# Spreading a statistics stream over sixteen turns of an image instead of twelve

## The chip, the cores and the metric

The kernel runs on one core of a Trainium2 chip. The metric is the device time of one execution in microseconds (us). The kernel before takes 6187.13 us, the median of 3 runs (6186.45 to 6190.99).

## The reference

The input x has 8 images of 32 channels by 512 by 512 pixels, float32. Two layers follow one another, each of the form x + layer(group norm of x); a group is two channels.

```python
def _gn(v, G=16, eps=1e-5):
    g = v.reshape(B_, G, C_ // G, H_, W_)
    m = jnp.mean(g, axis=(2, 3, 4), keepdims=True)
    s = jnp.var(g, axis=(2, 3, 4), keepdims=True)
    return ((g - m) / jnp.sqrt(s + eps)).reshape(v.shape)

# layer 0: 3x3 convolution on values quantised to int8, result quantised again
x_q = _quantize(x, S_X)
w_q = _quantize(weight, S_W)
acc = conv(x_q, w_q, padding=1)
out_q = clip(round((acc * (S_X * S_W) + bias) / S_OUT))      # times S_OUT
x = x + layer0(_gn(x))

# layer 1: 1x1 convolution, 5x5 pooled bins of it are the filter of a 5x5 depthwise convolution
x = x + layer1(_gn(x))
```

The mean and variance of a whole image must be known before the first value of this image can be quantised. That is why the first layer reads most of x twice.

## The kernel before, in words

The first layer is `quantised_conv`. An image is cut into N = 16 chunks of 2.1 MB (128 partitions by 8 rows by 512 float32), and one pass of a loop over n is a turn. Images are worked one after the other (`Fori` over b, the last image written out behind the loop). In turn n:

- SyncE (SP) and ScalarE (ACT) each issue the loads of half a chunk (L326) into one of eight slots `b_x`; a load waits until the store of the chunk that had the slot is complete. SP's loads run five turns ahead, and from n = 11 on they are chunks 0 to 5 of the next image.
- ACT quantises a chunk (L386), widens it to bf16 (L393) and rounds four results of the convolution (L401) into `b_q`, which has room for one chunk.
- TensorE (PE) does the convolution (L443 to L456).
- VectorE (DVE) adds the rounded result to the chunk (L521, two instructions), takes statistics of the sum for the second layer (L532, L536), and GpSimd (POOL) stores the chunk (L577).
- For the group norm of the next image, DVE takes bn_stats of its chunks too (L480). Four of its chunks (`RESIDENT`) are in their slots by then and are read there in turns 11 to 14. The other twelve are loaded once for this alone, by SP (L366), into `b_stream`, two halves of half a chunk each. A half is loaded again when DVE has read it. `TAKEN` says that these twelve are read in turns 0 to 11, one each.

In turn 14 the statistics are complete: DVE aggregates them (L484), PE sums over the partitions of a group (L255) behind its last convolution of the image, DVE forms spread and variance (L234 to L241), ACT a square root (L259) behind its last rounding of the image, DVE the scale (L490) and the shift (L491). The first L386 of the next image waits for L491. Behind turn 15 stands DVE's tail of an image (L542 to L554) with 20 chained links, each an instruction that waits for the one before it.

The order of the work is that of the code: each engine does its instructions in the order in which its loop issues them, and waits in between on semaphores. SP is one such queue for both kinds of load. DVE's add in turn n waits for ACT's rounding, ACT's next rounding waits for DVE's add, PE waits for ACT. The second layer (`depthwise`) begins when the first is over; the change doesn't touch it.

Of the kernel before, what the change touches and what calls it, by code (L numbers as in the profile page):

```python
# [27 lines left out]
RESIDENT = 4  # L28
XQ_SLOTS = 4
# [232 lines left out]
def quantised_conv(nc, nb, k, x, x1, own, sums):  # L262
# [4 lines left out]
    with ExitStack() as ctx:  # L267
        def sb(name, shape, dt):
            return ctx.enter_context(nc.sbuf_tensor(name, shape, dt))
# [8 lines left out]
        st_x = sb("b_stats_x", [P, N * JB, 6], F32)  # L278
        st = sb("b_stats", [P, NTUP, 6], F32)
# [34 lines left out]
        next_x = x[1:nb, :, :, :].rearrange("b c (n j r) w -> b n r c j w", j=JB, r=4)  # L314
        x1v = x1.rearrange("b (n j r) c w -> b n (r c) j w", j=JB, r=4)
# [28 lines left out]

        TAKEN = [[RESIDENT + n] if n < STREAMED else [] for n in range(N)]
        for j in range(RESIDENT):
            TAKEN[N - X_SLOTS + 3 + j].append(j)

        block = ctx.enter_context(nc.Block())

        @block.sync
        def _(sp):
            sem.start(sp)
            sp.wait_ge(padded, 1 + START)

            load_first(sp, (0, 1))

            def body(b, more):
                for n in range(N + 1):
                    load_ahead(sp, b, n + X_SLOTS - 3, more, (0, 1))  # L360
                    if more and n < STREAMED:
                        for h in range(2):

                            sp.wait_ge(stream_read[h], b * STREAMED + n + START)
                            for r in range(Q):
                                sp.dma_start(xs[C * r:C * r + C, h, :, :],  # L366
                                             next_x[b, RESIDENT + n, r, :, JB // 2 * h:JB // 2 * (h + 1), :]).then_inc(stream_loaded[h], 16)


            sp.wait_ge(first_read, N - AHEAD + START)  # L370
            with sp.Fori(0, nb - 1) as b:
                body(b, True)
            body(nb - 1, False)
# [96 lines left out]
        def _(dve):  # L470
# [4 lines left out]
            TAIL = 2 + 2 * NSEG + 1  # L475

            def take(tile, n, j0, rows):

                for j in range(rows):
                    last = dve.bn_stats(st_x[:, n * JB + j0 + j, :], tile[:, j, :])  # L480
                return last

# [10 lines left out]
            def body(b, more):  # L493
                tail = [0]

                def link(ins):
                    tail[0] += 1
                    ins.then_inc(chain, 1)
                    dve.wait_ge(chain, b * TAIL + tail[0] + START)

                for n in range(N):
                    s = n % X_SLOTS
                    for m in TAKEN[n] if more else ():
                        if m < RESIDENT:
                            dve.wait_ge(x_loaded[m], loads_at(b + 1, m) + START)
                            last = take(xt[:, m, :, :], m, 0, JB)
                        else:
                            for h in range(2):
                                dve.wait_ge(stream_loaded[h], b * (STREAMED * LOAD) + (m - RESIDENT + 1) * LOAD + START)
                                take(xs[:, h, :, :], m, JB // 2 * h, JB // 2).then_inc(stream_read[h], 1)  # L510
# [28 lines left out]
                    if more and n == N - 2:  # L539
                        gs.vector_variance(dve, b + 1)  # L540
# [16 lines left out]
            for i, n in enumerate([*range(AHEAD, N), *range(AHEAD)]):  # L557
                dve.wait_ge(x_loaded[n % X_SLOTS], LOAD * (i // X_SLOTS + 1) + START)
                last = take(xt[:, n % X_SLOTS, :, :], n, 0, JB).then_inc(first_read, 1)
# [5 lines left out]
            with dve.Fori(0, nb - 1) as b:  # L565
                body(b, True)
            body(nb - 1, False)
# [595 lines left out]
```

## Time and profile before

| | |
|---|---|
| median of 3 runs | 6187.13 us |
| the profiled execution, its time | 6187.55 us |
| its span in the profile | 6185.9 us |
| busy: PE, DVE, ACT, POOL | 79%, 85%, 54%, 14% |
| first image: scale known (L491) | at 129.9 us |
| last image: scale known | at 2323.0 us |
| last L386 of the first layer | starts at 2492.3 us |
| DVE, waiting for `b_stream` (L480) | 381.0 us in 151 waits |
| POOL, waiting in front of its stores (L577) | 2310.3 us |

The profiled execution took 0.4 us more than the median. Its span leaves out 1.65 us before and behind. The first layer fills about the first 42% of the span; the whole-span shares mix it with the second layer. So the first layer is read by stretches of an image.

### The profile page before, as it was taken

How to read it: one execution, taken by the hardware profiler on the slowest of the kernel's cores; microseconds unless marked ns; L12 is line 12 of the kernel's file. 1: busy time of each engine (PE TensorE's matmuls, PEld its weight loads, DVE VectorE, ACT ScalarE, POOL GpSimd, SP SyncE). 2: the span in 40 equal slices, each digit the busy share in tenths (PEclk: the TensorE clock that was granted, in tenths of full speed). 3: DMA queues.
4: the chain of work that ended last, by engine and by line, in shares of the span. 5: the costliest groups of instructions: out<-in, count | busy, mean ns of one | idle time of the engine just before them, and what ended most of it. 6: DMA issues, size and time to landing. Idle time of an engine off the chain costs nothing.

```text
span 6185.9 us, 112158 instructions
## 1 busy us (share of the span) xinstructions
PE 4916.9 (79%) x43630; PEld 3222.5 (52%) x43798; DVE 5284.7 (85%) x5934; ACT 3360.9 (54%) x2005; POOL 889.3 (14%) x1444
## 2 busy tenths in 40 slices
PE   1767676767676779349989989989899899899899
PEld 0111111111111112138878878878788788788787
DVE  6787878787878787659989989989899899899898
ACT  1656565646564649235545545545455455455454
POOL 0000000000000001102212212112112121122122
PEclk9888788878888889679999999999999999999999
DMA  8999999999999999389999999999999999999998
GB/s 259 301 280 307 287 300 287 303 286 294 299 301 298 297 286 299 100 182 257 244 251 251 250 252 252 251 249 257 246 260 243 256 255 250 256 249 251 252 255 195
DMA packets 617611, 1615.46 MB, mean 261 GB/s; under 512 B 81338, under 2 KB 82618, under 8 KB 580282
## 3 DMA queue, kind: packets, MB, share of 16 engines
q1 hardware_dynamic: 239298, 640.73, 41.7%
q0 software_dynamic: 162240, 537.03, 27.1%
q10 hardware_dynamic: 215488, 429.94, 25.8%
q8 instruction: 363, 5.95, 0.4%
q14 instruction: 222, 1.82, 0.1%
HBM read 1068.55 MB, written 538.84 MB: 260 GB/s over the span
## 4 chain that ended last, share of the span: by engine, by line
DVE 43%; issue 7%; DMA 3%; PE 2%; ACTq 1%; POOL 0%; SPq 0%; ACT 0%; DVEq 0%; another core or an unknown queue 0%; POOLq 0%
DVE c_z L1003 16%; DVE c_xr L1039 16%; DVE c_feat L1029 12%; DMA c_xr<-x_scratch 3%; PE c_tps L1083 1%; ACTq L859 1%; PE c_cps L1063 0%; POOL c_feat L922 0%; SPq L887 0%; PE c_cps L1065 0%; PE c_cps L1064 0%; ACT c_z L969 0%; DVEq L1002 0%; SPq L872 0%
## 5 line engine op out<-in xcount | busy, mean ns | idle before, releaser
L1083 PE MATMUL c_tps<-c_feat,c_tt 123*128 123x256 f16 (+1 forms) x20736 | 2377.0, 273 | 13.8 <-DVE c_xr L1039 10.7
L1083 PEld LDWEIGHTS c_tps<-c_feat,c_tt 123*128 123x128 f16 (+1 forms) x20736 | 1992.1, 97 | 275.0 <-issue 15.6
L987 ACT ACTIVATE c_feat<-c_cps 122x1024 f16<-122x1024 f32 x576 | 822.5, 1428 | 1352.1 <-PE c_cps L1065 1352.1
L1039 DVE SCALAR_TENSOR_TENSOR c_xr<-c_tps,c_xr 57x1024 f32<-57x1024 f32 (+1 forms) x1152 | 1403.2, 1218 | 158.6 <-DMA c_xr<-x_scratch 125.7
L443 PE MATMUL b_ps<-b_xq,w0main 128*128 128x512 bf16 x2904 | 918.4, 419 | 656.9 <-ACT b_q L401 484.5
L969 ACT ACTIVATE c_z<-c_x,c_rs 128x976 f16<-128x976 f32 x576 | 1156.6, 2008 | 275.5 <-PE c_tps L1083 169.1
L1003 DVE SCALAR_TENSOR_TENSOR c_z<-c_x,c_rs,c_z 128x976 f16<-128x976 f32 x576 | 1087.1, 1887 | 105.3 <-ACT c_z L969 92.9
L1063 PE MATMUL c_cps<-w_high,c_z 128*128 128x128 f16 x4608 | 822.1, 222 | 421.5 <-DVE c_z L1003 385.6
L936 POOL DMA_DIRECT2D out_dram<-c_xr x1152 | 667.4, 580 | 2892.5 <-DVE c_xr L1039 2827.9
L401 ACT ACTIVATE b_q<-b_ps,q_bias 128x1024 int8<-128x1024 f32 x512 | 549.2, 1115 | 813.8 <-DVE b_x L521 745.5
L456 PE MATMUL b_ps<-b_xq,w0edge 64*32 64x512 bf16 x3048 | 931.3, 416 | 0.0
L453 PE MATMUL b_ps<-b_xq,w0edge 64*32 64x512 bf16 x3048 | 929.3, 416 | 0.0
L443 PEld LDWEIGHTS b_ps<-b_xq,w0main 128*128 128x128 bf16 x3072 | 227.1, 101 | 1307.9 <-issue 1055.2
L1029 DVE TENSOR_TENSOR c_feat<-c_cps,c_feat 122x1024 f16<-122x1024 f32 x576 | 815.7, 1416 | 33.2 <-issue 12.1
L1064 PE MATMUL c_cps<-w_low,c_z 128*128 128x128 f16 x4608 | 816.7, 221 | 0.0
L1065 PE MATMUL c_cps<-w_high,c_z 128*128 128x128 f16 x4608 | 816.6, 221 | 0.0
L480 DVE BATCH_NORM_STATS2 b_stats_x<-b_stream 128x6 f32<-128x512 f32 x672 | 414.6, 681 | 410.3 <-DMA b_stream<-in_x_dram 381.0
L1063 PEld LDWEIGHTS c_cps<-w_high,c_z 128*128 128x128 f16 x4608 | 454.9, 99 | 572.5 <-DVE c_z L1003 556.1
L532 DVE BATCH_NORM_STATS2 b_stats<-b_x 128x6 f32<-128x408 f32 (+5 forms) x1520 | 645.4, 501 | 3.9
L521 DVE SCALAR_TENSOR_TENSOR b_x<-b_q,b_x 128x2048 f32<-128x2048 int8 x256 | 574.8, 2281 | 60.9 <-ACT b_q L401 60.9
L453 PEld LDWEIGHTS b_ps<-b_xq,w0edge 64*32 64x32 bf16 x3048 | 215.3, 96 | 621.1 <-issue 519.8
L386 ACT ACTIVATE b_x<-b_x,b_shift,b_scale 128x4096 int8<-128x4096 f32 x128 | 487.1, 3805 | 84.1 <-issue 57.7
(129 smaller groups left out, 2267.0 us busy)
## 6 DMA issues: line engine op xcount, KB each, us to landing
x_scratch<-b_x POOLq DMA_DIRECT2D x256, 1024.0 KB, 12.3
c_xr<-x_scratch SPq DMA_DIRECT2D x576, 384.0 KB
out_dram<-c_xr POOLq DMA_DIRECT2D x576, 384.0 KB, 7.9
b_stream<-in_x_dram SPq DMA_DIRECT2D x672, 256.0 KB, 12.4
b_x<-in_x_dram ACTq DMA_DIRECT2D x276, 512.0 KB, 13.6
b_x<-in_x_dram SPq DMA_DIRECT2D x276, 512.0 KB, 11.7
c_tt<-table_scratch SPq DMA_DIRECT2D x64, 576.0 KB
c_xr<-x_scratch SPq DMA_DIRECT2D x512, 72.0 KB
```

The costliest lines, as they stand in the source:

```text
L443: return pe.matmul(ps[:, g % 3, j, :], k.w0main[:, d, :, :].rearrange("p r o -> p (r o)"), xq[:, n % XQ_SLOTS, 2 * i + j, d:d + W], start= ...
L453: pe.matmul(ps[0:C, g % 3, j, :], k.w0edge[P // 2:P, d, :], xq[P // 2:P, (m - 1) // JB % XQ_SLOTS, (m - 1) % JB, d:d + W], start=False, st ...
L456: pe.matmul(ps[P - C:P, g % 3, j, :], k.w0edge[0:P // 2, d, :], xq[0:P // 2, (m + 1) // JB % XQ_SLOTS, (m + 1) % JB, d:d + W], start=False ...
L969: act.activation(split_part(0, part), positions(e, j, part), ACT.Identity, scale=scale_of(e, j)).then_inc(zh_done, 1)
L987: act.activation(dst, cps[0:MAIN, s % 2, :, :].rearrange("p j (q o) -> p o q j", q=Q), ACT.Identity).then_inc(fh_done, 1)
L1003: dve.scalar_tensor_tensor(split_part(1, part), positions(e, j, part), scale_of(e, j), split_part(0, part), ALU.mult, ALU.subtract).then_i ...
L1029: dve.tensor_tensor(lo, cps[0:MAIN, s % 2, :, :].rearrange("p j (q o) -> p o q j", q=Q), hi, ALU.subtract).then_inc(fl_done, 1)
L1039: last = dve.scalar_tensor_tensor(res, tps[PR * h:PR * h + n, s % 2, :, :], 1.0 / FS, res, ALU.mult, ALU.add)
L1063: pe.matmul(dst, zh, wh, start=True, stop=False)
L1064: pe.matmul(dst, zh, wl, start=False, stop=False)
L1065: last = pe.matmul(dst, zl, wh, start=False, stop=True)
L1083: last = pe.matmul(tps[:, s % 2, o % 4, :], tt[0:rows, o, tp, 2 * d:2 * d + 2, :].rearrange("k w m -> k (w m)"), feat[0:rows, (e * N + i) ...
```

## The change: what it does

Of the twelve streamed chunks of an image, four (`EARLY`) are now loaded and read in turns 12 to 15 of the image *two* places back. Their statistics go to a tile of their own, `b_stats_early` (128 x 192 float32), since `b_stats_x` is still in use for the image in between, and are copied over in turn 0 of the image one place back. The other eight (`LATE`) are read there, in turns 0, 1, 3, 4, 6, 7, 9 and 10; turns 2, 5, 8 and 11 carry none. For image 1, the four early chunks are loaded and read ahead of image 0's turns. Image 7's predecessor, image 6, has late chunks and no early ones. Two more edits go with it: the variance and the scale (`vector_variance`, `new_scales`) stand in turn 14, directly behind the spread, in place of behind the statistics of turn 14 and the adds of turn 15; and of the 20 links in the tail of an image 17 are dropped, since the 18 small reductions don't depend on each other. The loop runs over six images, and two are written out behind it.

```diff
-        TAKEN = [[RESIDENT + n] if n < STREAMED else [] for n in range(N)]
-        for j in range(RESIDENT):
-            TAKEN[N - X_SLOTS + 3 + j].append(j)
+        LATE = STREAMED - EARLY
+        LATE_AT = {n * (N - EARLY) // LATE: n for n in range(LATE)}
+        EARLY_AT = {N - EARLY + k: k for k in range(EARLY)}
+        RESIDENT_AT = {N - X_SLOTS + 3 + j: j for j in range(RESIDENT)}
...
+        def load_stream(eng, xv, i, t, k):
+            for h in range(2):
+                eng.wait_ge(stream_read[h], nth_stream(t, k) + START)
+                for r in range(Q):
+                    eng.dma_start(xs[C * r:C * r + C, h, :, :],
+                                  xv[i, RESIDENT + k, r, :, JB // 2 * h:JB // 2 * (h + 1), :]).then_inc(stream_loaded[h], 16)
...
-            def body(b, more):
+            def body(b, more, early):
                 for n in range(N + 1):
                     load_ahead(sp, b, n + X_SLOTS - 3, more, (0, 1))
-                    if more and n < STREAMED:
...
+                    if more and n in LATE_AT:
+                        load_stream(sp, next_x, b, b + 1, EARLY + LATE_AT[n])
+                    if early and n in EARLY_AT:
+                        load_stream(sp, after_x, b, b + 2, EARLY_AT[n])
+
+            for k in range(EARLY):
+                load_stream(sp, next_x, 0, 1, k)
             sp.wait_ge(first_read, N - AHEAD + START)
...
+            def take_stream(t, k, into, n):
+                for h in range(2):
+                    dve.wait_ge(stream_loaded[h], (nth_stream(t, k) + 1) * LOAD + START)
+                    take(xs[:, h, :, :], into, n, JB // 2 * h, JB // 2).then_inc(stream_read[h], 1)
...
                 for n in range(N):
+                    if more and n == 0:
+                        dve.wait_ge(stream_read[1], nth_stream(b + 1, EARLY) + START)
+                        dve.tensor_copy(st_x[:, RESIDENT * JB:(RESIDENT + EARLY) * JB, :], st_early[:, :, :])
+                    if more and n in LATE_AT:
+                        k = EARLY + LATE_AT[n]
+                        take_stream(b + 1, k, st_x, RESIDENT + k)
+                    if more and n in RESIDENT_AT:
...
                         means(b + 1)
+                    if early and n in EARLY_AT:
+                        k = EARLY_AT[n]
+                        take_stream(b + 2, k, st_early, k)
...
                     if more and n == N - 2:
                         gs.vector_spread(dve, b + 1, mv_x)
-                    if more and n == N - 1:
+                        gs.vector_variance(dve, b + 1)
                         new_scales(b + 1)
...
-                    link(dve.tensor_reduce(seg[:, m, 0:NBINS], cm[:, :, g0:g1, :], axis=AX.XY, op=ALU.add))
-                    link(dve.tensor_reduce(seg[:, m, NBINS:], cols[:, :, j0:j1], axis=AX.X, op=ALU.add))
+                    dve.tensor_reduce(seg[:, m, 0:NBINS], cm[:, :, g0:g1, :], axis=AX.XY, op=ALU.add)
+                    last = dve.tensor_reduce(seg[:, m, NBINS:], cols[:, :, j0:j1], axis=AX.X, op=ALU.add)
+                link(last)
...
+            for k in range(EARLY):
+                take_stream(1, k, st_early, k)
```

On DVE, turn 13 of an image before (from the reading of resident chunk 2 to the statistics of the sum):

```order
L480 BN_STATS b_stats_x<-b_x 128x6 [waits b_x_loaded2]
L480 BN_STATS b_stats_x<-b_x 128x6 x7
L519 REGISTER_ALU
L521 SCALAR_TENSOR_TENSOR b_x<-b_q,b_x 128x2048 [waits b_out_rounded]
L519 REGISTER_ALU
L521 SCALAR_TENSOR_TENSOR b_x<-b_q,b_x 128x2048 [waits b_out_rounded]
L526 REGISTER_ALU
L532 BN_STATS b_stats<-b_x 128x6 [waits b_added]
```

and the same turn now:

```order
L495 BN_STATS b_stats_x<-b_x 128x6 [waits b_x_loaded2]
L495 BN_STATS b_stats_x<-b_x 128x6 x7
L501 ISA
L495 BN_STATS b_stats_early<-b_stream 128x6 [waits b_stream_loaded0]
L495 BN_STATS b_stats_early<-b_stream 128x6 x3
L495 BN_STATS b_stats_early<-b_stream 128x6 [waits b_stream_loaded1]
L495 BN_STATS b_stats_early<-b_stream 128x6 x3
L546 REGISTER_ALU
L548 SCALAR_TENSOR_TENSOR b_x<-b_q,b_x 128x2048 [waits b_out_rounded]
L546 REGISTER_ALU
L548 SCALAR_TENSOR_TENSOR b_x<-b_q,b_x 128x2048 [waits b_out_rounded]
L553 REGISTER_ALU
```

Eight bn_stats of a streamed chunk, in two halves with a wait each, now stand between the resident chunk's and the adds; so it is in turns 12, 14 and 15 too.

On DVE, turn 14 behind the adds, before:

```order
L234 COPY b_gs_mean<-b_ps_g 128x1 [waits b_gs_product_done]
L226 ISA
L235 TENSOR_TENSOR b_gs_spread<-b_gs_own_mean,b_gs_mean 128x1 [waits b_gs_chain]
L226 REGISTER_ALU
L236 TENSOR_TENSOR b_gs_spread<-b_gs_spread 128x1 [waits b_gs_chain]
L226 REGISTER_ALU
L237 TENSOR_TENSOR b_gs_spread<-b_gs_spread,b_mv_x 128x1 [waits b_gs_chain]
L526 REGISTER_ALU
L532 BN_STATS b_stats<-b_x 128x6 [waits b_added]
L532 BN_STATS b_stats<-b_x 128x6 x9
L536 COPY b_cols<-b_x 128x2x8 x2
L240 REGISTER_ALU
```

and now, from the last instruction of the spread on:

```order
L238 TENSOR_TENSOR b_gs_spread<-b_gs_spread,b_mv_x 128x1 [waits b_gs_chain]
L241 REGISTER_ALU
L242 TENSOR_SCALAR b_gs_spread<-b_ps_g 128x1 [waits b_gs_product_done]
L247 RECIPROCAL b_gs_half<-b_gs_root 128x1 [waits b_gs_root_done]
L227 REGISTER_ALU
L248 TENSOR_TENSOR b_gs_half<-b_gs_half,b_gs_spread 128x1 [waits b_gs_chain]
L227 REGISTER_ALU
L249 TENSOR_TENSOR b_gs_half<-b_gs_half,b_gs_root 128x1 [waits b_gs_chain]
```

The variance waits for PE and the reciprocal for ACT with the statistics of turn 14 still to be done behind them; before, these stood in between.

On SP, the end of an image before has only loads of `b_x`:

```order
L326 ISA [waits b_x1_stored2]
L326 DMA b_x<-in_x_dram 32x8x512
L326 ISA
L326 DMA b_x<-in_x_dram 32x8x512
L326 ISA [waits b_x1_stored3]
L326 DMA b_x<-in_x_dram 32x8x512
L326 ISA
L326 DMA b_x<-in_x_dram 32x8x512
```

and now the loads of a streamed chunk stand between two of them (here the second half of one, which waits for DVE's reading):

```order
L362 ISA [waits b_stream_read1]
L362 DMA b_stream<-in_x_dram 32x4x512
L362 ISA
L362 DMA b_stream<-in_x_dram 32x4x512
L362 ISA
L362 DMA b_stream<-in_x_dram 32x4x512
L362 ISA
L362 DMA b_stream<-in_x_dram 32x4x512
L329 ISA [waits b_x1_stored3]
L329 DMA b_x<-in_x_dram 32x8x512
L329 ISA
L329 DMA b_x<-in_x_dram 32x8x512
```

A load of a `b_x` chunk at the end of an image is now queued behind the wait for a read of `b_stream`.

## Rows read from the trace of the kernel before

**Rows 1.** The page's 40 slices: DMA busy in tenths.

```profile
DMA  8999999999999999389999999999999999999998
```

**Rows 2.** Stretches: length, busy us of PE, PEld, DVE, ACT, POOL, clock, DMA share, GB/s.

```profile
1095.54:1292.65 197.11, 142.98 (x741) 36.86 (x749) 145.43 (x242) 117.40 (x61) 14.97 (x20) 0.86 1.05 311
1292.65:1316.68 24.03, 14.05 (x70) 3.58 (x72) 19.17 (x32) 11.54 (x6) 1.49 (x2) 0.82 1.03 344
1316.68:1410.88 94.20, 60.50 (x300) 16.36 (x305) 83.18 (x152) 51.00 (x28) 7.50 (x10) 0.76 0.82 241
130.00:150.00 20.00, 11.88 (x50) 2.81 (x51) 4.86 (x9) 19.44 (x6) 0.00 (x0) 1.00 0.77 158
150.00:170.00 20.00, 19.35 (x116) 5.55 (x118) 15.51 (x23) 20.00 (x12) 1.57 (x2) 1.00 0.44 110
2344.15:2524.00 179.85, 176.65 (x1054) 50.01 (x1073) 145.75 (x241) 159.13 (x87) 20.97 (x28) 1.00 0.79 270
```

**Rows 3.** DVE in order of time, one turn with a streamed chunk: start, us, instruction, [idle].

```profile
1112.90 4.47 DVE L521 SCALAR_TENSOR_TENSOR b_x<-b_q,b_x 128x2048 f32<-128x2048 int8 x2
1117.41 4.93 DVE L532 BATCH_NORM_STATS2 b_stats<-b_x 128x6 f32<-128x408 f32 x10
1122.26 0.24 DVE L536 COPY b_cols<-b_x 128x16 f32<-128x16 f32 x2
1125.74 2.47 DVE L480 BATCH_NORM_STATS2 b_stats_x<-b_stream 128x6 f32<-128x512 f32 x4 [3.24 <-DMA b_stream<-in_x_dram]
1130.25 2.47 DVE L480 BATCH_NORM_STATS2 b_stats_x<-b_stream 128x6 f32<-128x512 f32 x4 [2.04 <-DMA b_stream<-in_x_dram]
```

**Rows 4.** Waits of all engines over the span: us in total, times, longest.

```profile
DVE b_stats_x L480 <- DMA b_stream<-in_x_dram: 381.0, 151, 6.0
```

**Rows 5.** DVE in order of time, the streamed chunk of turn 11.

```profile
1304.71 2.47 DVE L480 BATCH_NORM_STATS2 b_stats_x<-b_stream 128x6 f32<-128x512 f32 x4 [2.47 <-DMA b_stream<-in_x_dram]
1309.54 2.47 DVE L480 BATCH_NORM_STATS2 b_stats_x<-b_stream 128x6 f32<-128x512 f32 x4 [2.36 <-DMA b_stream<-in_x_dram]
```

**Rows 6.** DVE and ACT in order of time, turns 14 and 15 of an image.

```profile
1057.04 0.16 DVE L234 COPY b_gs_mean<-b_ps_g 128x1 f32<-128x1 f32 x1 [3.79 <-PE b_ps_g L255]
1057.72 4.93 DVE L532 BATCH_NORM_STATS2 b_stats<-b_x 128x6 f32<-128x408 f32 x10
1062.79 4.48 DVE L521 SCALAR_TENSOR_TENSOR b_x<-b_q,b_x 128x2048 f32<-128x2048 int8 x2
1068.35 0.16 DVE L491 SCALAR_TENSOR_TENSOR b_shift<-b_gs_mean,b_scale 128x1 f32<-128x1 f32 x1
1068.71 3.80 ACT L386 ACTIVATE b_x<-b_x,b_shift,b_scale 128x4096 int8<-128x4096 f32 x1 [5.60 <-DVE b_shift L491]
```

**Rows 7.** DVE and ACT in order of time, the first image's scale and first add.

```profile
126.92 0.16 DVE L241 TENSOR_SCALAR b_gs_spread<-b_ps_g 128x1 f32<-128x1 f32 x1 [0.68 <-PE b_ps_g L255]
127.17 1.28 ACT L259 ACT_TABLE_LOAD   x1 [115.04 <-DVE b_gs_spread L241]
128.70 0.16 DVE L246 RECIPROCAL b_gs_half<-b_gs_root 128x1 f32<-128x1 f32 x1 [1.61 <-ACT b_gs_root L259]
130.06 4.84 DVE L480 BATCH_NORM_STATS2 b_stats_x<-b_stream 128x6 f32<-128x512 f32 x8
151.24 2.29 DVE L521 SCALAR_TENSOR_TENSOR b_x<-b_q,b_x 128x2048 f32<-128x2048 int8 x1 [16.33 <-ACT b_q L401]
```

**Rows 8.** DVE in order of time, two linked reductions of a tail.

```profile
1081.10 0.16 DVE L552 TENSOR_REDUCE b_seg<-b_cm 128x5 f32<-128x10 f32 x1
1081.30 0.16 DVE L553 TENSOR_REDUCE b_seg<-b_cols 128x4 f32<-128x4 f32 x1
```

**Rows 9.** L536, the unlinked copies: duration ns minimum, median, maximum.

```profile
L536 DVE COPY b_cols<-b_x x256: 151/163/174, 163.9 to 2535.9; 128x16 f32<-128x16 f32 x128
```

**Rows 10.** DMA issues from 132 to 150 us: count, KB each, median us to landing.

```profile
b_stream<-in_x_dram SPq DMA_DIRECT2D x8, 256.0 KB, 6.1
```

**Rows 11.** The same from 1110 to 1290 us.

```profile
b_stream<-in_x_dram SPq DMA_DIRECT2D x73, 256.0 KB, 13.0
```

**Rows 12.** DVE in order of time, the last image's scale and its first add.

```profile
2323.02 0.16 DVE L491 SCALAR_TENSOR_TENSOR b_shift<-b_gs_mean,b_scale 128x1 f32<-128x1 f32 x1
2344.15 2.29 DVE L521 SCALAR_TENSOR_TENSOR b_x<-b_q,b_x 128x2048 f32<-128x2048 int8 x1 [4.29 <-ACT b_q L401]
```

More of the change, by code:

```diff
@@ L28 @@
 RESIDENT = 4
+EARLY = 4
 XQ_SLOTS = 4
@@ L278, in quantised_conv @@
         st_x = sb("b_stats_x", [P, N * JB, 6], F32)
+        st_early = sb("b_stats_early", [P, EARLY * JB, 6], F32)
         st = sb("b_stats", [P, NTUP, 6], F32)
@@ L314, in quantised_conv @@
         next_x = x[1:nb, :, :, :].rearrange("b c (n j r) w -> b n r c j w", j=JB, r=4)
+        after_x = x[2:nb, :, :, :].rearrange("b c (n j r) w -> b n r c j w", j=JB, r=4)
         x1v = x1.rearrange("b (n j r) c w -> b n (r c) j w", j=JB, r=4)
@@ L343, in load_ahead, with nth_stream @@
                 load_chunk(eng, next_x, b, m - N, rows)
-        TAKEN = [[RESIDENT + n] if n < STREAMED else [] for n in range(N)]
-        for j in range(RESIDENT):
-            TAKEN[N - X_SLOTS + 3 + j].append(j)
+        LATE = STREAMED - EARLY
+        LATE_AT = {n * (N - EARLY) // LATE: n for n in range(LATE)}
+        EARLY_AT = {N - EARLY + k: k for k in range(EARLY)}
+        RESIDENT_AT = {N - X_SLOTS + 3 + j: j for j in range(RESIDENT)}
+        def nth_stream(b, k):
+            return (b - 1) * STREAMED + k
+        def load_stream(eng, xv, i, t, k):
[4 more added lines that the diff above has]
+                                  xv[i, RESIDENT + k, r, :, JB // 2 * h:JB // 2 * (h + 1), :]).then_inc(stream_loaded[h], 16)
         block = ctx.enter_context(nc.Block())
@@ L356, in _ @@
             load_first(sp, (0, 1))
-            def body(b, more):
+            def body(b, more, early):
                 for n in range(N + 1):
                     load_ahead(sp, b, n + X_SLOTS - 3, more, (0, 1))
-                    if more and n < STREAMED:
[L362 to L367, printed above, removed]
+                    if more and n in LATE_AT:
[4 more added lines that the diff above has]
+                load_stream(sp, next_x, 0, 1, k)
             sp.wait_ge(first_read, N - AHEAD + START)
-            with sp.Fori(0, nb - 1) as b:
-                body(b, True)
-            body(nb - 1, False)
+            with sp.Fori(0, nb - 2) as b:
+                body(b, True, True)
+            body(nb - 2, True, False)
+            body(nb - 1, False, False)
         @block.scalar
@@ L474, in _, with take @@
             last.then_inc(padded, 1)
-            TAIL = 2 + 2 * NSEG + 1
-            def take(tile, n, j0, rows):
+            TAIL = 4
+            def take(tile, into, n, j0, rows):
                 for j in range(rows):
-                    last = dve.bn_stats(st_x[:, n * JB + j0 + j, :], tile[:, j, :])
+                    last = dve.bn_stats(into[:, n * JB + j0 + j, :], tile[:, j, :])
                 return last
+            def take_stream(t, k, into, n):
+                for h in range(2):
+                    dve.wait_ge(stream_loaded[h], (nth_stream(t, k) + 1) * LOAD + START)
+                    take(xs[:, h, :, :], into, n, JB // 2 * h, JB // 2).then_inc(stream_read[h], 1)
             def means(t):
@@ L491, in new_scales, with body @@
                 dve.scalar_tensor_tensor(shift[:, :], gs.mean[:, :], -1.0, scale[:, :], ALU.mult, ALU.mult).then_inc(scales, 1)
-            def body(b, more):
+            def body(b, more, early):
                 tail = [0]
@@ L502, in body @@
                     s = n % X_SLOTS
[L503 to L510, printed above, removed]
+                    if more and n == 0:
[5 more added lines that the diff above has]
+                    if more and n in RESIDENT_AT:
+                        m = RESIDENT_AT[n]
+                        dve.wait_ge(x_loaded[m], loads_at(b + 1, m) + START)
+                        last = take(xt[:, m, :, :], st_x, m, 0, JB)
                     if more and n == N - 2:
@@ L538, in body @@
                     last.then_inc(measured, 1)
-                    if more and n == N - 2:
-                        gs.vector_variance(dve, b + 1)
                 dve.wait_ge(measured, b * N + N + START)
@@ L558, in _ @@
                 dve.wait_ge(x_loaded[n % X_SLOTS], LOAD * (i // X_SLOTS + 1) + START)
-                last = take(xt[:, n % X_SLOTS, :, :], n, 0, JB).then_inc(first_read, 1)
+                last = take(xt[:, n % X_SLOTS, :, :], st_x, n, 0, JB).then_inc(first_read, 1)
             dve.wait_ge(first_read, N + START)
@@ L564, in _ @@
             new_scales(0)
-            with dve.Fori(0, nb - 1) as b:
-                body(b, True)
-            body(nb - 1, False)
+            for k in range(EARLY):
+                take_stream(1, k, st_early, k)
+            with dve.Fori(0, nb - 2) as b:
+                body(b, True, True)
+            body(nb - 2, True, False)
+            body(nb - 1, False, False)
         @block.gpsimd
```

## The prediction, made before the changed kernel was run

> **What bounds the kernel now.** I read the page's slices first, since a whole-span share mixes two layers: in the first layer the DMA engines are busy at nine tenths nearly throughout [rows 1]. Then the starts of the adds (L521) of image 3, the fourth, as cuts for a table by stretch [rows 2]. An image falls into three parts. From the add of turn 0 to that of turn 10 (197.1 us, ten turns) the DMA share is 1.05, the table's full value, and DVE is busy only 145.4 us. From there to the add of turn 11 it is 24.0 us. From the add of turn 11 to the next image's first (94.2 us) the DMA share is 0.82 and DVE is busy 83.2 us. So the bound changes hands within an image: DMA for eleven turns, DVE for the end.
>
> One turn of the first part shows how DVE feels it [rows 3]: adds 4.5, statistics 5.2 with the copies, then each half of the streamed chunk is waited for (3.2 and 2.0 us) and read (2.5 each). That is 14.6 us of work in a turn of 19.7. Such waits sum to 381 us over the first layer [rows 4].
>
> First adds lie at 151.24 us (image 0) and 2344.15 us (image 7) [rows 7, 12]: seven periods of 313.3 us. What isn't named below, the second layer among it, I leave as it is.
>
> **The change part by part: a period (images 1 to 5).**
> *Turns 0 to 10.* A chunk is 128 x 4096 float32, 2.10 MB. Ten turns with load, stream and store move 62.9 MB in 197.1 us, 319 GB/s by my count. Turns 2, 5 and 8 lose their stream: 3 x 2.10 MB at 319 GB/s = 19.8 us less, if DMA stays the bound. It does by count: DVE needs 14.6 us in a streamed turn and 9.7 in a bare one; PE and ACT did bare turns in about 12 in the last image (179.85 us from its first add to its sixteenth, the granted clock at full [rows 2]). That is far below DMA's 13.1 and 19.7. So -19.8.
> *Turn 11* loses its stream: two waits of 2.47 and 2.36 and two reads of 2.47, less an overlap of 0.1 [rows 5]: -9.7. The resident chunk stays.
> *Turns 12 to 15* each gain a read of 4.84, the eight bn_stats of a chunk [rows 7]. DVE is the bound here, so it counts in full: +19.4. The transfers should hide: turn 12 or 13 becomes 19.2 to 19.7 us of DVE work, and DMA's share of a turn with all three transfers is 19.7; a half is asked for again when read, some 17 us before it is wanted (adds 4.5, statistics 5.2, resident 4.8, the other half 2.4), against 13.0 to land [rows 11]. Queued behind that wait on SP are the `b_x` loads of the next image; they are wanted over a turn later, so I put them at nothing. If the cover goes, see the slower rival.
> *Scale in turn 14.* DVE now waits for PE's second product, 0.68 us, and for the root: 1.61 less a table load of 1.28 that happens once, 0.33 [rows 7]. +1.0; the chain behind is only moved. ACT gets the scale earlier (in the old order it idled 5.60 us for it [rows 6]), but DVE is the late one at the image's change: worth nothing until the last image. What would be late next is DVE itself.
> *Tail.* Two linked reductions of 0.16 start 0.20 apart [rows 8]; two unlinked copies of 0.163 end within 0.24 [rows 3, 9], thus start 0.08 apart. 17 links x 0.12 = -2.0. The copy of `b_stats_early` has no row; between 0.1 and 0.7 us, I take 0.3.
> The end so makes +18.7. A period: -19.8 - 9.7 + 18.7 = -10.8; five of them, -54.
>
> The Trainium skill, "VectorE: DVE Perf Modes", section "The DRAIN you can't avoid", says otherwise on the links: it states that leaving out the semaphores between Vector instructions saves nothing. The rows disagree (0.20 against 0.08 us); by the page 8 x 2.0 = 16 us of the gain would be missing, giving 6121.
>
> **Image 0.** The four early chunks of image 1 are read before its turns. The first is there, as now [rows 7]. Each further one is asked for when the last is read and lands 6.1 us after its issue in a quiet stretch [rows 10]; with issue and reading some 10 us a round. So the first add falls not at 151 but near 177: three early rounds and one late. That alone costs 26. But DMA now works where it was idle (share 0.77 and 0.44 from 130 to 170 [rows 2]), and DMA bounds what follows: up to turn 10 it has one chunk more to move (+6.6 us) and gains up to the idle 13 to 17 us of that stretch. Between -6 and +8 at the add of turn 10; I take 0, in place of -19.8. With -9.7 and +18.7 this period costs +9.
>
> **Image 6 and the last.** Image 6 has no early chunks, so it has -19.8 and -9.7, and its end doesn't grow. The last image has neither stream nor next loads: DMA share 0.79, PE busy 176.7 of 179.9 us [rows 2], so it is paced by PE from the scale on. Its scale comes earlier by the statistics and adds that now stand behind it: from the start of the statistics to L491 it was 10.6 us [rows 6], now the two waits and the chain between [rows 7], some 2.9: 8. DVE frees itself later than PE's first results (these come 21 us behind the scale [rows 12]), so I count 6 of the 8. Tail of the last: -2. Together -37.5.
>
> **Sum.** +9 - 54 - 37.5 = -82.5. From the profiled 6187.55 us this is 6105; the median was 0.4 lower, which I neglect.
>
> **Rivals.**
> *Slower: the end becomes DMA's.* At turns 12 to 15 a stream is added where SP must also bring the next image. In turn 11 of the old kernel DVE waited 4.8 us for its two halves although they had been asked for 12 us earlier [rows 5]. If each of the four new reads waits 4.6 us, that is 18.4 a period, 110 over six: 6215. It turns the sign from 82.5 / 24 = 3.4 us a streamed turn on. For it: streams land in 13.0 us only in the median [rows 11], and the bare turns leave a backlog of loads. Against: 17 us are given now, and DMA had 0.82 in this part [rows 2].
> *Faster: bare turns outrun DMA.* `b_x` loads run turns ahead, and could slip in turns 0 to 10 and catch up at the end. A triple of turns then takes 12.8 + 14.6 + 19.7 = 47 in place of 52.5 us: 17 less a period, seven times, 5986. Against: 56.6 MB in 160 us are 354 GB/s, and 319 is what all of this part moved; the end has little idle left to catch up in. Half of it, 6045, is thinkable.
> The Trainium skill, "DMA: Bandwidth & Descriptors", its opening table, puts the HBM limit of a core at about 358 GB/s. An estimate by that page: nothing would forbid this rival. The row of the first part shows 311 with loads and stores mixed, so I don't use the page's figure.
> *The bare turns don't shorten.* If the 19.7 us of a turn are latency in a ring of waits (store, load behind it on SP, stream behind both) rather than DMA's throughput, a bare turn stays near 19: seven periods lose 19.8 each, 6244, or half of it and no change. Against: bare turns drop exactly the wait that DVE shows, and SP's stream loads in turn 3 wait for the store of turn 0, which is complete by turn 2.
>
> **How the numbers follow.** Forecast, 6105, 0.62; for it I give 6080 to 6140 (image 0 by 8 either way, the bare turns by 2 a period, small waits in the end of up to 1 a turn). Faster rival, in part or whole, 0.16. Slower rival in full or half (6160 still counts as faster), 0.14. Bare turns staying, 0.08. The 0.2% about what this measurement can tell from no change, is 12.4 us. Faster by more (below 6175): 0.62 + 0.16 + 0.05 of the partial cases = 0.83. Slower (above 6199.5): 0.12. Same: 0.05. The range of 8 in 10 reaches from half the faster rival to half the slower one with a little over: 6045 to 6170.
>
> **What would show it.** In the profile after: intervals between adds near 13 (bare) and 17 to 20 (streamed) with their DMA share still 1.05 over turns 0 to 10, sum near 177; 14.4 into turn 11; 19.2, 19.7, 23, 22 and 29.5 in the end; DVE's wait for `b_stream` down by about a quarter to a third; first add near 177 us; the period near 302. I am wrong if turns 12 to 15 show waits for `b_stream` of over 3 us each, if the reads of resident chunks wait for `b_x`, or if the first part moves far more than 320 GB/s.

## The result, and the profile after

The changed kernel takes 6273.68 us (median of 4 runs, 6267.3 to 6285.17) against 6186.79 us for the kernel before (4 runs): ratio 1.0145, 95% interval 1.0125 to 1.0166. It is slower by 87 us where 82 us less had been forecast. The profiled execution took 6285.17 us.

Image 2 of the changed kernel by stretch answers to the first three lines of [rows 2] (there image 3; the periods of images 1 to 5 lie from 310.5 to 319.4 us before and from 325.6 to 331.5 after): turns 0 to 10, the way to the add of turn 11, the end.

```profile
842.38:1035.60 193.22, 128.26 (x710) 33.84 (x709) 130.04 (x218) 113.89 (x60) 14.97 (x20) 0.83 1.00 276
1035.60:1049.90 14.30, 13.10 (x79) 3.57 (x75) 14.27 (x24) 8.51 (x6) 1.50 (x2) 1.00 0.86 281
1049.90:1172.16 122.26, 74.32 (x367) 19.37 (x366) 101.16 (x185) 60.52 (x32) 7.48 (x10) 0.76 1.02 287
```

Turns 0 to 10 carry three chunks less and last 193 us, hardly less than before. DMA is still busy at a share of 1.00 and moves only 276 GB/s. Turn 11 came out as forecast (14.3), the end 9 us longer (113 forecast). In the end of this image DVE waited for a DMA in turn 12 alone, for the early chunk and for the resident one. The prediction had named both as signs of being wrong. DVE's waits from 1049 to 1172 us:

```profile
DVE b_stats_early L495 <- DMA b_stream<-in_x_dram: 5.2, 1, 5.2
DVE b_stats_x L495 <- DMA b_x<-in_x_dram: 3.5, 1, 3.5
```

The first image: three early rounds of about 10 us, as worked out, the copy of 0.26 us, and the first add at 183.71 (forecast 177); the round of the late chunk took 14 us. The lines show the last early round and the copy.

```profile
161.36 2.47 DVE L495 BATCH_NORM_STATS2 b_stats_early<-b_stream 128x6 f32<-128x512 f32 x4 [3.52 <-DMA b_stream<-in_x_dram]
171.16 2.47 DVE L495 BATCH_NORM_STATS2 b_stats_early<-b_stream 128x6 f32<-128x512 f32 x4 [7.33 <-DMA b_stream<-in_x_dram]
173.67 0.26 DVE L527 COPY b_stats_x<-b_stats_early 128x192 f32<-128x192 f32 x1
183.71 4.47 DVE L548 SCALAR_TENSOR_TENSOR b_x<-b_q,b_x 128x2048 f32<-128x2048 int8 x2
```

DVE's waits for the stream, against [rows 4]: 74 waits in place of 151, of 6.8 us in the mean in place of 2.5. In total they rose from 381 to 504 us, where the forecast had them fall by a quarter to a third.

```profile
DVE b_stats_x L495 <- DMA b_stream<-in_x_dram: 441.0, 61, 18.1
DVE b_stats_early L495 <- DMA b_stream<-in_x_dram: 63.1, 13, 7.9
```

Where they sit shows in DVE's turns 0 to 3 of image 1 (answer to [rows 3]; turn 2 is bare):

```profile
514.74 4.47 DVE L548 SCALAR_TENSOR_TENSOR b_x<-b_q,b_x 128x2048 f32<-128x2048 int8 x2
...
524.25 4.84 DVE L495 BATCH_NORM_STATS2 b_stats_x<-b_stream 128x6 f32<-128x512 f32 x8
529.00 4.48 DVE L548 SCALAR_TENSOR_TENSOR b_x<-b_q,b_x 128x2048 f32<-128x2048 int8 x2
...
538.52 4.48 DVE L548 SCALAR_TENSOR_TENSOR b_x<-b_q,b_x 128x2048 f32<-128x2048 int8 x2
...
564.00 2.47 DVE L495 BATCH_NORM_STATS2 b_stats_x<-b_stream 128x6 f32<-128x512 f32 x4 [15.88 <-DMA b_stream<-in_x_dram]
571.99 2.47 DVE L495 BATCH_NORM_STATS2 b_stats_x<-b_stream 128x6 f32<-128x512 f32 x4 [5.52 <-DMA b_stream<-in_x_dram]
574.38 4.47 DVE L548 SCALAR_TENSOR_TENSOR b_x<-b_q,b_x 128x2048 f32<-128x2048 int8 x2
```

The adds are 14.3, 9.5 and 35.9 us apart: three turns take 59.6 us, before they took about 59 (the mean of images 1 to 5). DVE gains in two turns and gives all back in the third. SP's queue in the same time, in order of issue:

```profile
512.62 4.18 SPq L362 DMA_DIRECT2D b_stream<-in_x_dram  x8
516.98 24.54 SPq L329 DMA_DIRECT2D b_x<-in_x_dram  x4
541.77 7.98 SPq L362 DMA_DIRECT2D b_stream<-in_x_dram  x8
```

Of the four `b_x` loads in the middle, merged into one line, the last two are those of turn 3. A view from 530 us on has them alone:

```profile
540.24 1.28 SPq L329 DMA_DIRECT2D b_x<-in_x_dram  x2
```

POOL's stores in the same time:

```profile
525.00 1.49 POOL L606 DMA_DIRECT2D x_scratch<-b_x  x2 [27.59 <-DVE b_cols L563]
539.25 1.49 POOL L606 DMA_DIRECT2D x_scratch<-b_x  x2 [12.76 <-DVE b_cols L563]
548.77 1.50 POOL L606 DMA_DIRECT2D x_scratch<-b_x  x2 [8.03 <-DVE b_cols L563]
```

DVE had read the first half by 526.7, but the load of the next chunk is issued at 541.8: in front of it on SP stands the `b_x` load that waits for the store issued at 525.0. By then two stores and the `b_x` loads of both queues come at once, and the half lands 22 us after its issue.

### The profile page after: what moved, and what is told of

Read it like the earlier page. It is cut to its first block, busy times and chain, and to the rows that moved or that the text cites. A ratio compares the mean times of both kernels' runs of the same rounds, so it can differ in the third digit from the quotient of the medians.

```text
span 6283.5 us, 111893 instructions
## 1 busy us (share of the span) xinstructions
PE 4887.3 (78%) x43798; PEld 3221.8 (51%) x43798; DVE 5268.2 (84%) x5941; ACT 3359.3 (53%) x2005; POOL 888.6 (14%) x1444
## 4 chain that ended last, share of the span: by engine, by line
DVE 43%; issue 7%; DMA 3%; PE 2%; ACTq 1%; POOL 0%; SPq 0%; DVEq 0%; ACT 0%; another core or an unknown queue 0%; POOLq 0%
DVE c_xr L1068 16%; DVE c_z L1032 16%; DVE c_feat L1058 12%; DMA c_xr<-x_scratch 3%; PE c_tps L1112 1%; ACTq L888 1%; PE c_cps L1092 0%; POOL c_feat L951 0%; SPq L916 0%; PE c_cps L1094 0%; PE c_cps L1093 0%; ACT c_z L998 0%; DVEq L1031 0%; POOL c_starter L948 0%
## 5 line engine op out<-in xcount | busy, mean ns | idle before, releaser
L1112 PEld LDWEIGHTS c_tps<-c_feat,c_tt 123*128 123x128 f16 (+1 forms) x20736 | 1994.6, 97 | 279.7 <-issue 18.7
L471 PE MATMUL b_ps<-b_xq,w0edge 64*32 64x512 bf16 x3048 | 894.6, 403 | 0.0
L468 PE MATMUL b_ps<-b_xq,w0edge 64*32 64x512 bf16 x3048 | 892.7, 402 | 0.0
L1058 DVE TENSOR_TENSOR c_feat<-c_cps,c_feat 122x1024 f16<-122x1024 f32 x576 | 816.6, 1418 | 25.5 <-ACT c_feat L1016 7.8
L495 DVE BATCH_NORM_STATS2 b_stats_x<-b_stream 128x6 f32<-128x512 f32 x448 | 275.0, 679 | 441.0 <-DMA b_stream<-in_x_dram 441.0
L606 POOL DMA_DIRECT2D x_scratch<-b_x x256 | 191.6, 753 | 2426.5 <-DVE b_cols L563 2408.4
```

The lines of the kernel that those rows point to most:

```text
L468: pe.matmul(ps[0:C, g % 3, j, :], k.w0edge[P // 2:P, d, :], xq[P // 2:P, (m - 1) // JB % XQ_SLOTS, (m - 1) % JB, d:d + W], start=False, st ...
L471: pe.matmul(ps[P - C:P, g % 3, j, :], k.w0edge[0:P // 2, d, :], xq[0:P // 2, (m + 1) // JB % XQ_SLOTS, (m + 1) % JB, d:d + W], start=False ...
L1058: dve.tensor_tensor(lo, cps[0:MAIN, s % 2, :, :].rearrange("p j (q o) -> p o q j", q=Q), hi, ALU.subtract).then_inc(fl_done, 1)
L1112: last = pe.matmul(tps[:, s % 2, o % 4, :], tt[0:rows, o, tp, 2 * d:2 * d + 2, :].rearrange("k w m -> k (w m)"), feat[0:rows, (e * N + i) ...
```

## The experiments

Ratios are to the kernel before on the same chip. "Intervals" are the distances of the adds in an undisturbed image; "slow full" is the time of a period in which DMA is busy at nine tenths or more and moves under 260 GB/s (slices of 1.5 us, images 2 to 4 of each trace): 117 us before, 161 after.

**e1, the two small edits alone** (before, with `vector_variance` and `new_scales` in turn 14 and the links dropped).

> The kernel before with two of the change's edits alone: variance and scale in turn 14 behind the spread, and 17 links of the tail dropped; the streamed chunks stay in turns 0 to 11. By the terms of the prediction: +1.0 and -2.0 us a period, 8 us less in the last image: about 6170. If these edits carry the loss (a wait of DVE for the square root that grows), 6187 plus up to 87.

6162.6 us, ratio 0.9967 (0.9956 to 0.9978), faster by 22. They don't carry the loss. The 18 reductions took 2.1 us from first start to last end where they had taken 4.3. The first interval of an image fell from about 18 to 15 us: that I had put at nothing. Before, DVE waited in this interval for the two halves of the stream; in e1 these waits are short or gone. Image 3 before, and then in e1:

```profile
1105.62 2.48 DVE L480 BATCH_NORM_STATS2 b_stats_x<-b_stream 128x6 f32<-128x512 f32 x4 [0.49 <-DMA b_stream<-in_x_dram]
1110.52 2.47 DVE L480 BATCH_NORM_STATS2 b_stats_x<-b_stream 128x6 f32<-128x512 f32 x4 [2.42 <-DMA b_stream<-in_x_dram]
```

```profile
1094.19 5.07 DVE L480 BATCH_NORM_STATS2 b_stats_x<-b_stream 128x6 f32<-128x512 f32 x8
```

ACT, which has the scale earlier, issued its `b_x` loads 5.8 us ahead of the first add there in place of 3.3, and the stream's DMAs, issued at the same place (2.1 us ahead of it), landed after 5.3 to 10.2 us in place of 7.9 to 12.8. That the one is the cause of the other is likely and not tested.

**e2, stream issued earlier** and **e17, only the late chunks earlier**. On SP:

```diff
+            ISSUE_AT = {0: 0, **{turns[i - 1] + 1: i for i in range(1, len(turns))}}
-                    if more and n in LATE_AT:
-                        load_stream(sp, next_x, b, b + 1, EARLY + LATE_AT[n])
+                    if more and n in ISSUE_AT:
+                        load_stream(sp, next_x, b, b + 1, EARLY + ISSUE_AT[n])
```

In e2 the four early chunks move up by one turn too, in e17 they stay.

> The changed kernel; on SyncE's queue the load of a streamed chunk that follows a bare turn, and of the four early ones, is issued one turn earlier, so that it no longer stands behind the b_x load that waits for the store of the turn just done. Theory Q (the order in SyncE's queue issues the stream 15 us late): the 35 us intervals behind a bare turn fall to 20 to 25, the wait of 9 us in turn 12 goes, a period loses some 20 us, 6120 to 6160. Theory R (SyncE's queue is worked off at about 200 GB/s when it is alone, and it has 42 MB an image): the transfers are the bound, the wait only moves to another turn, 6240 to 6280.

> The changed kernel, whole chunks, with only the eight late chunks issued early on SyncE's queue, right behind the turn that frees their buffer; the four early chunks stay at their own turns, so that the b_x loads of the image's end no longer stand behind a wait for DVE (in e2 DVE waited some 10 us for resident chunks there). Turns 0 to 10 as in e2 (183 us, against 193 in the changed kernel and 168 by halves), the end at 118 to 122: a period 316 to 320, 6180 to 6215. If it is 6240 or more, early issue of whole chunks is worth nothing and the halves carry all of e12's gain.

e2: 6251.7 us, 1.0114 (1.0087 to 1.014). e17: 6162.11 us, 0.9965 (0.9949 to 0.9981), below even its range. The late chunks of turns 3, 6 and 9 issued one turn earlier on one queue (the other five keep their place) are worth 112 us to the changed kernel. A period by stretch in e17:

```profile
808.77:991.20 182.43, 130.42 (x721) 34.42 (x720) 130.06 (x218) 113.56 (x60) 14.97 (x20) 0.86 1.04 310
1005.50:1119.18 113.68, 73.30 (x376) 19.55 (x375) 101.05 (x185) 57.80 (x31) 7.49 (x10) 0.79 1.02 292
```

The end is the forecast 112.9 to a microsecond. The long interval isn't gone, though: it moved by a turn. The means of images 1 to 5 for turns 3 and 4 were 35.3 and 14.9 us, in e17 they are 14.5 and 34.5. In turn 4 the stream's load (851.09 below) now stands behind the `b_x` load that waits for the store of turn 1, and DVE waits for it:

```profile
836.65 14.19 SPq L329 DMA_DIRECT2D b_x<-in_x_dram  x4
851.09 7.29 SPq L362 DMA_DIRECT2D b_stream<-in_x_dram  x8
```

```profile
873.88 2.47 DVE L498 BATCH_NORM_STATS2 b_stats_x<-b_stream 128x6 f32<-128x512 f32 x4 [16.62 <-DMA b_stream<-in_x_dram]
```

e2 has the same 181 to 184 for turns 0 to 10 but 123 to 130 for the end: its `b_x` loads of the resident chunks now stood behind SP's waits for DVE, which cost 9.0 and 7.4 us in one image:

```profile
1067.78 4.84 DVE L498 BATCH_NORM_STATS2 b_stats_x<-b_x 128x6 f32<-128x512 f32 x8 [9.03 <-DMA b_x<-in_x_dram]
1094.25 4.84 DVE L498 BATCH_NORM_STATS2 b_stats_x<-b_x 128x6 f32<-128x512 f32 x8 [7.36 <-DMA b_x<-in_x_dram]
```

So queueing in either direction on SP decides here.

**e3 and e4, all `b_x` loads of the loop on ACT**, in before and in the changed kernel (`load_ahead(act, ..., (0, 1, 2, 3))`, none on SP).

> The kernel before, with all four quarter loads of a b_x chunk issued by ScalarE behind the first image's loads, none by SyncE; SyncE then issues only the streamed chunks. Theory R: turns 0 to 10 are bound by SyncE's queue (2.1 MB of stream and 1.05 MB of b_x a turn); with a third of its bytes moved to the other queue the ten turns take 165 to 180 us in place of 196, 6000 to 6090. Theory Q: SyncE's order cost nothing in the kernel before, and the total of bytes is the bound: 6180 to 6195, or slower by ScalarE's issue time.

> The changed kernel with the same move of b_x loads to ScalarE. SyncE's stream loads then wait for DVE's reads alone. Theory Q: as with the streams issued earlier, 6120 to 6160. Theory R: the queue is relieved as well, below that: 5980 to 6080.

e3: 6264.2 us, 1.0116 (1.0089 to 1.0143); e4: 6186.38 us, 1.0008 (0.9993 to 1.0022). Taking bytes off SP's queue made the kernel before slower: theory R in this form fell, turns 0 to 10 took 197 to 208 us; why they grew isn't shown. The changed kernel gained 87 us, as Q said, since SP's streams wait for nothing but DVE's reads there; it stayed above Q's range. Its turns 0 to 10 last 173.0 us, 10 less than e17's and below the 177 of the forecast, but turn 11 takes 30 us for 14.3, since DVE waits there for a resident chunk, whose loads are all on ACT now:

```profile
810.98:983.97 172.99, 134.61 (x713) 35.19 (x726) 130.14 (x218) 111.23 (x60) 14.97 (x20) 0.88 1.05 321
```

```profile
1010.33 4.85 DVE L495 BATCH_NORM_STATS2 b_stats_x<-b_x 128x6 f32<-128x512 f32 x8 [16.77 <-DMA b_x<-in_x_dram]
```

**e5, both queues on the same partitions.** Each queue loads half the rows of a chunk in all four partition groups.

> The kernel before with the loads of b_x cut otherwise: SyncE loads rows 0 to 3 of a chunk in all four groups of 32 partitions, one after the other, ScalarE rows 4 to 7, in the same order; so both queues write the same 32 partitions at about the same time, where before SyncE wrote partitions 0 to 63 and ScalarE 64 to 127. Read in the first image's loads, 60 to 100 us, where nothing else runs (369 GB/s before). Theory P (the slow stretches of about 205 GB/s come from writing one group of 32 partitions at a time): about 205 GB/s here too, the first add 60 us or more later. Theory R (they come from one queue alone being at work): 350 to 370 GB/s as before.

6253.75 us in the one run that was made, and the first add 29 us later. The first image's loads, 60 to 100 us, of the kernel before:

```profile
60.00:100.00 40.00, 0.00 (x0) 0.00 (x0) 33.73 (x57) 0.00 (x0) 0.00 (x0) 1.00 1.05 369
```

and of e5:

```profile
60.00:100.00 40.00, 0.00 (x0) 0.00 (x0) 24.23 (x40) 0.00 (x0) 0.00 (x0) 1.00 1.07 272
```

Between both theories: the same bytes on the same two queues go at 272 in place of 369 GB/s when both work through the same groups of 32 partitions in the same order, at a DMA share as full. Each DMA is also half as large as before (four rows in place of eight).

**e7, e8, e9, e10, streams on both queues.** SP loads partitions 0 to 63 of a streamed half, ACT 64 to 127, at the end of ACT's turn:

```diff
+                    for r in (2, 3):
+                        act.dma_start(xs[C * r:C * r + C, h, :, :],
+                                      next_x[b, RESIDENT + n, r, :, JB // 2 * h:JB // 2 * (h + 1), :]).then_inc(stream_loaded[h], 16)
```

e7 is before with this, e8 with e1's edits too, e9 the changed kernel with it, e10 e9 with ACT's `b_x` loads in front of its wait.

> The kernel before with the streamed chunks' loads shared: SyncE loads partitions 0 to 63 of a half, ScalarE 64 to 127. Theory R or P: a lone stream load is no longer worked off at 205 GB/s but near 370; the 117 us of full-but-slow DMA a period (below 260 GB/s) fall under 60, turns 0 to 10 from 196 to 150 to 175 us, 5950 to 6080. Rival O (what counts is the bytes in the ring of waits, the rate of a lone load is a symptom of there being nothing else to move): no change, or slower by what ScalarE's waits for DVE's reads cost it: 6180 to 6260.

> As the kernel before with the streamed loads shared by both queues, and with the two edits (scale in turn 14, links dropped) on top, which brought 22 us alone. 15 to 25 us below e7 if the edits and the queues add.

> The changed kernel with its streamed loads shared by SyncE and ScalarE in the same way. Theory R or P: the slow full stretches (161 us a period) fall by more than half, the 35 us intervals behind bare turns shrink to about 20, a period 290 to 305 in place of 330, 6000 to 6110; if the spreading over sixteen turns is worth its 10 us a period once the transfers are fast, this is below e8. Rival O: stays within 1% of 6274, since the late issue of the stream is untouched for SyncE's half.

> As e9 (spread over sixteen turns, streams on both queues), with ScalarE's b_x loads of a turn issued in front of its wait for DVE's read of the stream. In e9 DVE waited 8, 4 and 6 us in turns 12 to 14 for resident chunks whose ScalarE half stood behind that wait. If that queueing is the loss, the end of an image falls from 128 to about 114 us and the time from 6110 to about 6020, below e8's 6065: the spreading pays once transfers are fast and queues don't block each other. If the transfers of the end collide anyway, it stays near 6100.

e7: 6081.69 us, 0.9829 (0.9807 to 0.9851). e8: 6064.9, 0.9794 (0.9774 to 0.9814). e9: 6109.85, 0.9871 (0.985 to 0.9891). e10: 6071.42, 0.9812 (0.9792 to 0.9832). Slow full time fell from 117 to 75 (e7) and from 161 to 65 (e9) us a period. e10 got its end back (112 us in place of 127), but its turns 0 to 10 are longer by some 8 us, so it gained 38 us, less than half of the 90 expected. The interval into turn 3 went from 20.1 to 28.7 us: ACT's half of the stream now stands behind its `b_x` loads, as SP's does. e8 and e10 can't be told apart by their intervals: with the streams on both queues, spreading whole chunks over sixteen turns is still worth nothing that can be told from zero.

**e11 and e16, finer loads on SP alone**, in before and in the changed kernel: a half as eight DMAs of two rows that cycle through the partition groups.

> The kernel before; the streamed chunks stay on SyncE's queue alone, but each half is loaded by eight DMAs of 32 partitions by 2 rows, cycling through the four groups of 32 partitions after every two rows in place of four. Theory P (one group of 32 partitions written at a time is what makes a lone stream slow): consecutive pieces go to different groups, the slow full stretches shrink, 6090 to 6160. Theory R (one queue alone is slow whatever it writes): no change or slower, 6180 to 6230.

> The changed kernel with nothing else changed than the eight smaller DMAs for each half. It has 161 us a period of full and slow DMA, more than the kernel before (117), so the finer loads should bring it more than the 53 us that they brought there: 6170 to 6210. If the late issue and the bare turns hold the time whatever the rate: 6240 to 6270.

e11: 6132.19 us, 0.9908 (0.9886 to 0.9929): with one queue and other pieces, 53 us less, slow full time 82 us a period. e16: 6268.36 us, 1.0144 (1.0112 to 1.0177): in the changed kernel the same finer loads bring nothing that can be told from zero, and the slow full time stays at 156 us a period. That the late issue holds the time there fits with e15 below, where finer loads bring 28 us once the issue is early, but it isn't shown by itself.

**e12, e14, halves.** The 16 halves of the late chunks are read one or two to a turn over turns 0 to 11, none is bare. In e12 a half is issued once its buffer was read, in e14 in the turn that reads it.

```diff
+        HALF_AT = [i * (N - EARLY) // (2 * LATE) for i in range(2 * LATE)]
+        ISSUE_AT = [0 if i < 2 else HALF_AT[i - 2] + 1 for i in range(2 * LATE)]
```

> The changed kernel on SyncE's queue alone, but the eight late chunks are read by halves, 16 halves over turns 0 to 11 as 2, 1, 1, and so on, so that no turn is bare, and each half is issued as soon as DVE has read its buffer. Theory G (bare turns bunch the stores, and then the streams are left alone on the DMA engines at 205 GB/s): intervals even out to 15 to 20 us, slow stretches fall from 161 to about 120 us a period, 6160 to 6200. If bunching is not the point but the bytes on SyncE's queue: near e2, 6240 to 6270.

> e12 with each half issued by SyncE in the turn that reads it, behind the b_x load of that turn, as in the changed kernel. If reading by halves is the cure: 6110 to 6140. If e12's gain was the early issue: back near 6230 to 6270.

e12: 6109.39 us, 0.9876 (0.9853 to 0.9899). e14: 6217.1, 1.0051 (1.0035 to 1.0067). Against the changed kernel: halves alone -57, early issue alone -112 (e17), both -164, nearly the sum. e14 lies between its two ranges. The intervals of e12 were no evener than before (11.9, 11.9, 27.9), so theory G's wording was wrong: the bunching stays, and most of the slow full time too (136 us a period). What changed is that DMA has a share of 1.05 and 316 GB/s in turns 0 to 10, for 1.00 and 276.

**e13 and e15, remedies together**: e12 with both queues as in e10, and e12 with e11's fine loads.

> Halves over turns 0 to 11 as in e12, early issue as there, and the loads of each half shared by SyncE and ScalarE with the b_x loads in front, as in e10. If the two remedies add (no bare turns; no lone slow stream), turns 0 to 10 go from 168 to 150 us and the end to 113: 5990 to 6030, the fastest so far. If DVE, PE and the ring of buffers are what is left, no better than e8 and e10: 6050 to 6075.

> e12 with each half loaded by eight DMAs of two rows that cycle through the four groups of partitions, all on SyncE. If the remedies add: e12's 6109 less e11's 53, about 6055. If SyncE's issue time (sixteen more DMAs of 0.34 us a chunk) or the bound of DVE eats it: 6090 to 6110.

e15: 6080.98 us, 0.9834 (0.9805 to 0.9864), 28 us below e12 where 53 would be the sum. e13: 5990.87 us, 0.9691 (0.9663 to 0.972), as expected, faster than both kernels by far and 74 us below e8, which streams in twelve turns. A kernel with twelve turns and an earlier issue wasn't run, so how much of these 74 us belongs to the spreading is open. Turns 0 to 10 and the end in e13:

```profile
754.76:909.10 154.34, 123.12 (x676) 32.42 (x676) 127.55 (x214) 113.11 (x60) 14.83 (x20) 0.88 1.04 343
928.80:1040.39 111.59, 69.85 (x349) 18.11 (x350) 100.93 (x185) 57.79 (x31) 7.49 (x10) 0.80 1.01 299
```

## Why the prediction was wrong

*The step that failed*: the term of turns 0 to 10, "19.8 us less, if DMA stays the bound", and with it the remark under the third rival that "SP's stream loads in turn 3 wait for the store of turn 0, which is complete by turn 2", by which this wait was put at nothing. The mean of images 1 to 5 went from 196.1 to 193.6 us: -2.5. It is the rival "the bare turns don't shorten" in effect, but not as I drew it: bare turns shortened fully, to 9.5 us, and the streamed turn behind each grew to 35. By the prediction's own intervals, 17 to 20 us and 13, the add of turn 2 comes 30 us or more after that of turn 0. It came after 23.8 us, with the store of turn 0 still in the air: the `b_x` load that waits for this store went out 25.5 us after the add of turn 0, and the stream's load behind it 15 us after its buffer was free. Two runs that change this queue alone or nearly so show the cause. In e17 three such loads are issued one turn earlier, with the same bytes and buffers: -112 us of the 169 between forecast and result. In e4 no `b_x` load stands in front of the stream at all: turns 0 to 10 fall to 172.9 us in the mean, 23 below the kernel before and 30 below e3, the kernel before with the same move, where 19.8 had been forecast. The late issue is not all of it: the DMAs of this chunk also took 15 to 24 us each to land, where 13.0 was the median before [rows 11]. With the streams on both queues, turns 0 to 10 go from 182.0 (e7) to 162.5 us (e9), which is -19.5 and as forecast, though SP's loads stand in the same order. Late issue and a slow lone queue make the loss together.

*The end* (+18.7 forecast, +27.3 measured on the mean of images 1 to 5): turns 13 to 15 and the tail were right to 1.5 us in images 1 to 4 (19.6, 22.9, 21 to 22, 29.4 after; forecast 19.7, 23, 22.3, 29.5). Only the interval into turn 12 was 28 to 31 for 19.2. It falls to 20 in e17, whose end is otherwise the same code, so it is not the slower rival's collision of transfers. It is the failed step once more: turn 12 follows a bare turn, and its early chunk is issued behind a `b_x` load that waits for the store of turn 9, at 1049 us in image 2, when the add of turn 11 was due. In e17 the long interval lies between the adds of turns 9 and 10, the store has landed by the add of turn 10, and the early chunk is issued 14 us ahead of the add of turn 11.

*The loop*: the interval from image 5 into image 6 was 24.0 in place of 29.4. In the changed kernel DVE idles 5.4 to 5.8 us with nothing to wait for ("issue") whenever another pass of the loop starts, and a loop over six images has one such start less than a loop over seven. The prediction had nothing for this.

*Turn 11* -9.4 (forecast -9.7). *Image 0*: first add at 183.7, not 177, and 31 us late at turn 10 where 0 was forecast: its turns 3, 6 and 9 show the same intervals of 34 us. *Image 6*: 287.3 us for 311.9, which is -24.6; forecast were -19.8, -9.7 and the 6 of the earlier scale, -35.5. *Scale*: DVE's wait for the root was 0.27 us for 0.33. That the earlier scale was worth nothing before the last image was wrong by 3 to 4 us a period (e1).

*Links*: 2.2 us saved, 2.0 forecast. The 18 reductions take 4.3 us before and 2.1 after. By a measurement that the section "The DRAIN you can't avoid" of the Trainium skill's page "VectorE: DVE Perf Modes" gives, with and without semaphores in the same time, it would be nothing; the same section also says that a next instruction that isn't held starts earlier, and with that the rows agree. Two unlinked reductions of the changed kernel, which answer to [rows 8], start 0.07 us apart:

```profile
830.00 0.15 DVE L578 TENSOR_REDUCE b_seg<-b_cols 128x4 f32<-128x4 f32 x1
830.07 0.22 DVE L577 TENSOR_REDUCE b_seg<-b_cm 128x5 f32<-128x70 f32 x1
```

*What I took for the bound.* I read the share of 1.05 as DMA being the bound, at 319 GB/s, and that hid that a full share has several rates. The 319 was itself a count of three transfers a turn; the view had 311. In e17 turns 0 to 10 move 310 GB/s, the rate of before, and last 182.4 us: about 5 MB less than before in this part, not the 6.3 MB of three chunks. So e17's last 5 us over the forecast of 177 come from the bytes and not from a slower rate. e13's gain over e17 in this part goes with a higher rate. The faster rival was thinkable after all: e13 moves 343 GB/s in its first part, once queues are shared. The 358 GB/s of the Trainium skill ("DMA: Bandwidth & Descriptors", opening table) lie above this stretch and all stretches of an image's turns 0 to 10, but the 40 us of loads at 369 in the kernel before (e5) and a stretch of 12 us below, at 407, lie above the page's figure, so here it was no ceiling. Not settled: how the two effects (one queue alone, one partition group at a time) share the slow rate; e5 and e11 each change the pieces of a transfer as well.

## What to carry to other kernels

When a change makes some turns shorter, ask for every in-order queue what stands in front of each transfer and when *that* will be free at the new pace; a wait that was always over can become the bound. A transfer is best issued where its buffer comes free and not where it is used (e17), as long as nothing that is wanted sooner is queued behind its wait (e2). And before a "full" DMA is taken as a bound, look at its GB/s in short slices: if these differ by a factor of two, as here, another mix of queues and partitions is worth a run (e7, -107 us).

## What the runs showed of the hardware

With SP's queue almost alone (stream loads of 256 KB and `b_x` loads of 512 KB, each into 32 partitions), DMA is full and slow; with stores and ACT's loads beside it DMA is full and fast. In the lines q1 is SP's queue, q10 ACT's and q0 that of POOL's stores: packets, MB, share of the engines. The changed kernel at 568 to 590 us:

```profile
DMA packets 2512, 4.71 MB, mean 214 GB/s; under 512 B 211, under 2 KB 211, under 8 KB 2512
q1 hardware_dynamic: 2209, 4.11, 92.9%
q10 hardware_dynamic: 303, 0.60, 13.7%
```

and at 550 to 562 us:

```profile
DMA packets 1911, 4.89 MB, mean 407 GB/s; under 512 B 144, under 2 KB 144, under 8 KB 1910
q0 software_dynamic: 651, 2.51, 51.9%
q1 hardware_dynamic: 707, 1.30, 28.3%
q10 hardware_dynamic: 552, 1.06, 23.0%
```

Both have a busy share of nine tenths or more in every slice. Two queues that load different partitions reach 369 GB/s; with the same partitions in the same order, and pieces half as large, 272 (e5).
